# Experts of the last batch in three token spans instead of two, with the whole step order written anew

## What is computed

```
x  = x + xattn0(x, ctx)              # 16 heads, softmax over 77 keys
s  = x @ Wr + br; top 2 of 8 experts, softmax of the two
x += sum_e w_e * (relu(x @ W1[e] + b1[e]) @ W2[e] + b2[e])       # 8 experts, H = 512
# layer 1, text block
sc = (q(x) @ k(ctx)) / sqrt(32)      # 4 heads, 77 keys
p  = softmax over the 32 largest of the 77; mean over heads
c  = p @ V                           # modulates the normalised x (FiLM)
y  = s4d(FiLM(layernorm(x)))         # a convolution over all 512 tokens, by DFT
x3 = x + FiLM(y); x5 = layernorm(x3 + gelu-ffn(layernorm(x3)))
out = x5 + quantized(layernorm(x5)) @ quantized(rhs)
```

## Time and profile before

| what | us |
|---|---|
| median of 3 runs | 533.92 |
| runs | 533.39 to 535.6 |
| the profiled execution, its own time | 530.86 |
| its span, first to last instruction | 529.0 |
| busy: TensorE | 464.2 (88%) |
| busy: VectorE | 422.4 (80%) |
| busy: ScalarE | 257.1 (49%) |
| busy: GpSimd | 118.0 (22%) |

### The profile page before, as it was taken

The page is one execution under the profiler, slowest core; times in us unless marked ns, Lnnn a source line. Parts: engine busy times, 40 slices in busy tenths (PEclk is TensorE's granted clock), DMA queues, the critical chain, the costliest instruction groups (busy, mean ns, idle before and its releaser), DMA issues.

```text
span 529.0 us, 9306 instructions
## 1 busy us (share of the span) xinstructions
PE 464.2 (88%) x3050; PEld 365.7 (69%) x3057; DVE 422.4 (80%) x1761; ACT 257.1 (49%) x548; POOL 118.0 (22%) x193
## 2 busy tenths in 40 slices
PE   4727578999999999999999999999999999758861
PEld 3316416899769989747988789759869888436750
DVE  4889997846337857978999998998798699995667
ACT  3626477754644565634447645543575434721040
POOL 6820113210200210004022243100225220342021
PEclk9968599999999999999999999999999999968996
DMA  7510293021000040000004000000000000000000
GB/s 202 67 30 2 71 334 102 2 40 22 2 2 2 1 60 1 4 2 0 2 1 60 2 1 1 24 1 1 1 2 2 4 18 2 0 1 21 1 0 20
DMA packets 16179, 14.69 MB, mean 28 GB/s; under 512 B 1211, under 2 KB 14275, under 8 KB 16132
## 3 DMA queue, kind: packets, MB, share of 16 engines
q1 hardware_dynamic: 16132, 14.11, 11.7%
HBM read 8.79 MB, written 1.05 MB: 19 GB/s over the span
## 4 chain that ended last, share of the span: by engine, by line
PE 72%; DVE 18%; issue 3%; ACT 3%; POOL 3%; DMA 1%; DVEq 0%; POOLq 0%; ACTq 0%
PE moe_y L959 20%; PE moe_h L947 20%; PE side L1015 4%; PE side L904 3%; PE side L906 3%; PE side L1003 3%; PE side L1025 2%; PE side L1068 2%; PE side L1046 2%; DVE area L1452 2%; PE side L803 1%; PE side L983 1%; PE side L1034 1%; PE side L865 1%; PE moe_h L969 1%
## 5 line engine op out<-in xcount | busy, mean ns | idle before, releaser
L1179 ACT ACTIVATE HT<-moe_h,W 128x256 f32<-128x256 f32 x256 | 115.4, 473 | 103.0 <-PE moe_h L947 102.5
L947 PE MATMUL moe_h<-xnT_moe,W 128*128 128x256 f32 x512 | 136.4, 382 | 1.0 <-ACT xnT_moe L1121 0.8
L959 PEld LDWEIGHTS moe_y<-W,HT 128*128 128x128 f32 x1024 | 131.0, 191 | 8.7 <-issue 1.4
L959 PE MATMUL moe_y<-W,HT 128*128 128x128 f32 x1024 | 135.6, 276 | 0.2 <-DVE X L1425 0.2
L947 PEld LDWEIGHTS moe_h<-xnT_moe,W 128*128 128x128 f32 x512 | 87.5, 191 | 14.5 <-issue 6.9
L1425 DVE SCALAR_TENSOR_TENSOR X<-moe_y,RW,X 128x128 f32<-128x128 f32 x128 | 38.6, 345 | 12.9 <-PE moe_y L959 12.1
L1452 DVE MATCH_REPLACE8 area<-TOP,area 128x77 f32<-128x77 f32 x192 | 40.9, 231 | 0.0
L1756 POOL TENSOR_TENSOR area<-area 128x128 f32<-128x128 f32 x16 | 7.3, 458 | 109.9 <-ACT area L1209 109.9
L1439 DVE MAX8 TOP<-area 128x8 f32<-128x77 f32 x192 | 31.5, 231 | 0.0
L1366 DVE TENSOR_REDUCE mx<-side 128x6 f32<-128x462 f32 (+1 forms) x48 | 24.9, 579 | 8.1 <-PE side L865 8.1
L969 PE MATMUL moe_h<-W 128*128 128x256 f32 x112 | 30.0, 428 | 0.0
(11 more groups left out here) (325 smaller groups left out, 827.7 us busy)
## 6 DMA issues: line engine op xcount, KB each, us to landing
W<-in_w SPq DMA_DIRECT2D x8, 512.0 KB, 8.4
QA<-Q SPq DMA_DIRECT2D x24, 128.0 KB, 4.1
X<-in_x SPq DMA_DIRECT2D x4, 256.0 KB, 7.3
KM<-area SPq DMA_DIRECT2D x6, 160.0 KB, 5.2
out_dram<-FO SPq DMA_DIRECT2D x3, 256.0 KB, 2.3
V<-in_vpack SPq DMA_DIRECT2D x1, 579.0 KB, 9.7
area<-in_gpack SPq DMA_DIRECT2D x1, 576.0 KB, 6.0
FW<-in_dftf SPq DMA_DIRECT2D x1, 512.0 KB, 7.0
```

The source lines that it names most:

```text
L947: pe.matmul(moe_h[n % 2][:, 0:HS], W1[:, e, c * P:(c + 1) * P], xnT_moe[:, b % 2, h * HS:(h + 1) * HS], start=True, stop=True).then_inc(mo ...
L959: mm = pe.matmul(moe_y[m % 2][:, t * P:(t + 1) * P], HT[:, m % 2, c, t * P:(t + 1) * P], W2[:, e, c, :], start=(c == 0), stop=(c == HC - 1))
L1179: act.activation(HT[:, m % 2, c, :], moe_h[n % 2][:, 0:HS], ACT.Relu, bias=wc("b1")[:, e * HC + c:e * HC + c + 1]).then_inc(moe_h_ready, 1)
```

## The change

In the last batch the experts run over three token spans: tiles 0 and 1 as before, tile 2 alone, tile 3 alone. So the second half's 8 units of 256 tokens become 16 units of 128 tokens. Each of these has its own four chunks (weights loaded again, products of 128 columns), one `moe_down`, one addition. `text1` then covers tile 2 and a new `text2` tile 3, each with its own normalisation, query and semaphore counts. For a span of one tile `moe_steps` puts all four chunks in a row and then the one `moe_down`. The other batches keep their two halves. `ORDER` is another string, in all parts of the program. The counts of all other steps stay.

```diff
+def spans(b):
+    return [range(0, HT_), range(HT_, T)] if b < LAST else [range(0, HT_)] + [range(t, t + 1) for t in range(HT_, T)]
+def span_of(b, t):
+    return next(h for h, tiles in enumerate(spans(b)) if t in tiles)
+def columns(b, h):
+    return slice(spans(b)[h].start * P, spans(b)[h].stop * P)
 def moe_steps(b):
-    units = [(h, e) for h in range(HN) for e in range(E8)]
+    units = [(h, e) for h in range(len(spans(b))) for e in range(E8)]
     for n in range(len(units) + 1):
-        for t in range(HT_):
+        now = len(spans(b)[units[n][0]]) if n < len(units) else 0
+        past = len(spans(b)[units[n - 1][0]]) if n >= 1 else 0
+        parts = max(now, past)
+        for t in range(parts):
             if n < len(units):
-                out += [("moe_up", b, units[n] + (c,)) for c in range(t * HC // HT_, (t + 1) * HC // HT_)]
-            if n >= 1:
+                out += [("moe_up", b, units[n] + (c,)) for c in range(t * HC // parts, (t + 1) * HC // parts)]
+            if t < past:
                 out.append(("moe_down", b, units[n - 1] + (t,)))
...
 ORDER = """
-H S M S H K H3 K F H F H F3 M H4 K W K2 W K2 W6 K H K2 H K H2 K2 W H9 K H K H K H K4 W K H5 W4 K H E2 H E2 H2 K E5 H
+H S H M S W4 H2 K H F W2 K H F4 W M H4 K7 W2 H2 K W H K H4 K W H6 W K2 H4 K7 H W2 H K H3 K H K E2 H E2 H E5 H2 E K E
...
-TEXT = ["text" + str(h) for h in range(HN)]
+TEXT = ["text" + str(h) for h in range(HN + 1)]
...
     if kind == "ln_stats" and i in TEXT:
...
-        return [("text_q", b, t // HT_)] + ([("am_T", n // T, n % T)] if n >= 0 else []) if r == 0 else [former]
+        return [("text_q", b, span_of(b, t))] + ([("am_T", n // T, n % T)] if n >= 0 else []) if r == 0 else [former]
...
-                    pe.matmul(moe_h[n % 2][:, 0:HS], W1[:, e, c * P:(c + 1) * P], xnT_moe[:, b % 2, h * HS:(h + 1) * HS],
+                    pe.matmul(moe_h[n % 2][:, 0:len(spans(b)[h]) * P], W1[:, e, c * P:(c + 1) * P], xnT_moe[:, b % 2, columns(b, h)],
                               start=True, stop=True).then_inc(moe_h_full, 1)
...
-                    if t == HT_ - 1:
+                    if t == len(spans(b)[h]) - 1:
                         mm.then_inc(moe_y_full, 1)
...
-                    act.activation(HT[:, m % 2, c, :], moe_h[n % 2][:, 0:HS], ACT.Relu,
+                    act.activation(HT[:, m % 2, c, 0:len(spans(b)[h]) * P], moe_h[n % 2][:, 0:len(spans(b)[h]) * P], ACT.Relu,
...
-                    for k in range(HT_):
-                        t = h * HT_ + k
+                    for k, t in enumerate(spans(b)[h]):
                         ins = dve.scalar_tensor_tensor(X[:, b, t, :], moe_y[m % 2][:, k * P:(k + 1) * P],
```

72 lines of the change are left out of this document (39 added, 33 removed).

## The result

| | us |
|---|---|
| kernel before, median of 5 runs taken beside it | 533.39 |
| changed kernel, median of 5 runs | 550.53 (549.89 to 556.26) |
| ratio, 95% interval | 1.0342 (1.0309 to 1.0375) |
| forecast | 548.6 (539 to 557) |

The profiled execution of the changed kernel was the one of 556.26 us. So I ran the kernel once more without an edit and read that profile: its execution took 549.64, with a span of 547.8, beside 530.86 and 529.0 of the profile before.

The account below looks back on a forecast made before the run. VectorE was taken to bound the kernel up to 84 us, then TensorE, and after the change VectorE in the last batch: 530.86 + 24.6 to the last addition - 9.9 behind it = 545.6, plus 3.06 to the median, 548.6 us (539 to 557).

Parts of the forecast that it names:

- The front: Steps ahead of the first expert product: later kgen_base +6.8 us and kgen_mul +3.1, so that product starts +9.9 later.
- `kgen_mul` on the path: Third quarter's kgen_mul, now ahead of the o_proj addition on VectorE, delays the first expert product by 3.1 us.
- Between the front and the last batch: First expert product to last batch: TensorE saves 2.1 and 4.2 us, so the last batch starts at 369.7.
- The last batch: Experts over three spans: VectorE becomes the bound, last addition at 475.0 instead of 450.4, +24.6 us.
- VectorE's sum: VectorE's work in the last batch before the last addition: 103.1 us, against 99.8 for TensorE.
- My first rival: TensorE stays the bound in the last batch and VectorE's work doesn't bind: 543.1 us, chance 0.24.
- Narrow chunks: Last batch, TensorE: 64 chunks of 128 columns for 32 of 256 cost +0.3 us, weight loads staying hidden.
- Relu waits: Last batch, TensorE: runs of four chunks with two banks wait for relus, 8 units at 0.6, 4.8 us.
- The idle time that I left for VectorE: Last batch: of VectorE's 11.1 us idle before the change, 3.4 us remain.
- Behind the last addition: From the last addition to the last dft: rounds, topw and half a normalisation leave, -9.9 us, 24.3 for 34.2.
- The third rival: Tile 3's text chain ends later than tile 2's covering rounds, so the 9.9 us gain fails: 558.5 us, chance 0.08.
- Not slower: VectorE carries the time nowhere, before 84 us or in the last batch: 533.2 us, 529 with short relu waits, chance 0.12.

Follow-up runs that it names:

- the experiment that took 7.0 away: Changed kernel with the first kgen_base step moved ahead of the four warm steps, norm_T and q_proj: 546.41 us, ratio 1.0299.

## Why the prediction was right, point by point

**The time.** 548.6 was forecast and 550.5 came. The steps add up as follows, in the profile's own time: first expert product 100.9 forecast, 102.1 measured; last batch 369.7 and 374.2; last addition 475.0 and 482.0; from there to the `dft` 24.3 and 23.1; the last chain 44.4 and 42.7; span 543.7 and 547.8; profile to median 3.06, and 0.4 in the repeated run (549.64 to 550.05). Term by term the errors are +1.2, +3.3, +2.5, -1.2 and -1.7, and -2.7 from the profile to the median. Three terms too small by 7.0 in all were offset by three too large by 5.6, so that the total came within 2 us is partly luck.

**The front: place right, one term missing.** `kgen_base` was said to start at 23.0, with VectorE idle for 6 to 8 us ahead of it, released by L1248; it starts at 22.68, idle for 7.49. I said that nothing hides this. 1.3 of it were made up by `attn_sum`, and the experiment that took 7.0 away gained 4.5. `kgen_mul` on the path was put at 3.1 (2.8 to 3.7), and measured 2.9. So 8.1 came of 9.9 forecast. Missing was the sentence on `kgen_exp`: moving `kgen_mm` ahead releases it, and it then runs on GpSimd just as VectorE does the normalisation that everything waits for, at 2.6 us. It was in the change's list of steps, and the earlier trace rows even shows ScalarE waiting for GpSimd's earlier ones. I had asked of each moved step where its own engine stood and never what its neighbours were doing.

**Between the front and the last batch.** The sum was 268.8 and 272.1 was measured. TensorE's saved 2.1 and 4.2 are there, but the first expert products run at half rate (2.05 us for four instructions in place of 1.10). From the first product to the third expert it took 10.0 us, where it took 9.0 with 2.1 us more work in it. That is 3.1 us of the 3.3. Four warm steps had stood right ahead of these products. I priced them where they went, and not what they had kept up where they stood.

**The last batch: time nearly right, reason half wrong.** The step that failed is VectorE's sum. I put 103.1 us of work into 105.3 and called VectorE the bound of the whole batch, over 95% busy. It has 97.3 in 107.8, 90%, and the last addition came 7.0 late all the same. Of the surplus of 5.8, `s4_out` of batch 1 (1.4) and an addition (0.6) were counted twice, since they already stood in the 73.2 of the window before; the 1.6 us of `spectrum` done ahead of the batch I had taken off elsewhere, as 1.2; the rest, 2.2, I have not traced. What the runs show is two bounds one behind the other. Up to 438.3 it is TensorE, 63.0 busy of 64.1 us. From there to 482.0 it is VectorE, partly through ScalarE's queue: taking 4.1 us off VectorE gave 3.0, taking the relu waits off TensorE gave nothing, since waits for VectorE came in their place. My first rival, TensorE the bound throughout, is so right for the first 60% of the batch, and its time (543.1) came out too low because it left out what the span of tile 3 waits for, and the front's two missing terms.

**TensorE's terms.** Narrow chunks at +0.3: four instructions of a pair take 0.45 us (464.30 to 464.75 in the repeated run), 0.11 each with a weight load each, as forecast. The rule of the Trainium skill (TensorE: Matmul & The Clock Gate, The mechanism), by which a load overlaps running matmuls only when its rows differ, would by my estimate, with the P / 1.2 ns for a load of the section LDWEIGHTS (107 ns at 128 columns), have made it 0.22 each; the trace does not agree. The same section of the Trainium skill also names loads into a background weight buffer as pulled ahead of running matmuls; I had passed that over, and the hidden loads fit it. Relu waits at 4.8, from 0.6 for a run of four: a run costs 0.5, so some 4.3 for eight. The waits in the profile are another count: of their 3.9 us, 1.8 is behind ScalarE's exponential, which I had not foreseen. The idle time that I left for VectorE, 3.4, was in the trace 2.6 for GpSimd's root and 2.6 for scores. Of the first of these at most 1.4 was a cost of its own.

**Behind the last addition.** -9.9 forecast, -11.1 measured. The third rival (tile 2 stays on the path) is out: VectorE is busy 21.25 of 23.1 us there, and its only waits are two of 0.6 us for TensorE's steps of the quantised product, none for tile 3.

**The other rivals.** Not slower: it was to decide from a first product at 91.7 or earlier, and that came at 102.1. Without the front it would not have come true either: with the old front the changed kernel's shortest run took 539.8, and this rival had 533.2.

**What the change was worth without its front.** 11.1 us gained behind the last addition against 23.5 more ahead of it, of which by the forecast's count 10.4 are work that was moved (6.2 from behind, 4.2 from ahead). The spans alone, in the order of before, cost 11.2 us ahead of the addition. The forecast had 5.1 for them, with half of the units in runs.
